# Later batches' mamba with products over 2048 columns, three buffers of decays and two of results

## The reference

```python
x = x + tanh(g_xattn[0]) * mamba(ctx, z=layernorm(x), ...)     # layer 0, "mamba"
x = x + tanh(g_ffn[0]) * bit_linear_ffn(layernorm(x), ...)     # hidden 2048, quantised
x = x + tanh(g_xattn[1]) * attention(layernorm(x), ctx, ...)   # 16 heads of 128 a batch
x = x + tanh(g_ffn[1]) * experts(layernorm(x), ...)            # 4 experts
```

```python
delta = softplus(dt_proj_w @ dt_lo + dt_proj_b); A = -exp(A_log)
# per step t, channel e, state n
dA = exp(delta[e, t] * A[e, n])
state[e, n] = state[e, n] * dA + delta[e, t] * u[e, t] * B[n, t]
y[e, t] += state[e, n] * C[n, t]
y = (y + D * u) * silu(z)
```

## Time and profile before

| | us |
|---|---|
| median of three runs | 1851.22 |
| the profiled execution | 1852.26 |
| its span, first to last instruction | 1850.5 |
| TensorE busy | 1763.2 |
| VectorE busy | 1300.1 |
| ScalarE busy | 963.8 |
| GpSimd busy | 666.5 |

### The profile page before, as it was taken

How to read it: one execution, slowest core, us unless ns; L and a number is a source line. 1 busy time by engine, 2 the same in 40 slices (tenths; PEclk the granted TensorE clock), 3 DMA queues, 4 the chain that set the end, 5 groups by cost and what they waited for, 6 DMA issues and landing times.

```text
span 1850.5 us, 19507 instructions
## 1 busy us (share of the span) xinstructions
PE 1763.2 (95%) x6114; PEld 809.9 (44%) x6114; DVE 1300.1 (70%) x1899; ACT 963.8 (52%) x1920; POOL 666.5 (36%) x696
## 2 busy tenths in 40 slices
PE   8999899879999999999999999999999899999999
PEld 4333344334444444444444444444444344445543
DVE  4989686989998689899787998987652444422221
ACT  7988786446545546566455566555435334320100
POOL 2434322337463324557222564562223333310000
PEclk9999899979999999999999999999999999999999
DMA  7999833767851146897212589732112799837110
GB/s 262 242 289 286 244 109 116 203 164 187 199 142 57 51 100 162 208 240 200 66 30 74 156 188 251 199 95 69 35 57 91 218 282 293 236 119 273 40 51 28
DMA packets 159045, 292.11 MB, mean 158 GB/s; under 512 B 18424, under 2 KB 51704, under 8 KB 156000
## 3 DMA queue, kind: packets, MB, share of 16 engines
q1 hardware_dynamic: 141664, 227.95, 39.0%
q0 software_dynamic: 17280, 62.92, 17.5%
HBM read 169.51 MB, written 58.26 MB: 123 GB/s over the span
## 4 chain that ended last, share of the span: by engine, by line
PE 72%; DVE 13%; ACT 6%; issue 4%; DMA 3%; POOL 1%; SPq 1%; DVEq 0%; ACTq 0%; POOLq 0%
PE p L846 11%; PE p L806 10%; PE p L823 9%; PE p L857 8%; PE p L893 6%; PE p L697 5%; DVE s_M L1025 5%; PE p L780 4%; PE p L829 4%; PE p L908 3%; PE p L746 3%; PE p L785 3%; DVE s_M L1020 2%; DVE s_M L1032 1%; DVE s_U L1178 1%
## 5 line engine op out<-in xcount | busy, mean ns | idle before, releaser
L1025 DVE TENSOR_TENSOR_SCAN s_M<-s_M 128x1024 f32<-128x1024 f32 x128 | 296.4, 2315 | 9.9 <-ACT s_M L1290 7.6
L1178 DVE CUSTOM_DVE_ANT_0 s_U<-p,s_U 128x512 f32<-128x512 f32 x256 | 188.2, 745 | 161.0 <-PE p L823 159.7
L823 PE MATMUL p<-s_U 128*128 128x512 f32 x512 | 268.2, 612 | 4.6 <-DVE s_U L1178 3.0
L806 PE MATMUL p<-s_U 128*128 128x512 f32 x512 | 256.7, 610 | 3.4 <-ACT s_U L1418 2.7
L1534 POOL DMA_DIRECT2D s_u<-s_M x120 | 111.7, 931 | 383.7 <-DVE s_M L1032 355.6
L1579 POOL TENSOR_SCALAR s_U<-s_U 128x512 f32<-128x512 f32 x256 | 231.9, 926 | 6.3
L857 PE MATMUL p<-s_U 128*128 128x512 f32 x512 | 223.7, 593 | 0.0
L846 PE MATMUL p<-s_U 128*128 128x512 f32 x472 | 216.0, 599 | 2.5 <-ACT s_U L1431 2.4
L1431 ACT COPY s_U<-p 128x512 f32<-128x512 f32 x196 | 105.5, 594 | 176.3 <-PE p L829 175.0
L1290 ACT ACTIVATE s_M<-s_dl,s_small 128x511 f32<-128x511 f32 x256 | 170.3, 717 | 35.5 <-DVE s_M L1025 35.3
L1426 ACT ACTIVATE s_U<-s_U 128x512 f32<-128x512 f32 x256 | 181.6, 710 | 5.3
(11 more groups left out here) (194 smaller groups left out, 2458.3 us busy)
## 6 DMA issues: line engine op xcount, KB each, us to landing
s_u<-s_M POOLq DMA_DIRECT2D x120, 512.0 KB, 7.6
s_bc<-bc_scratch SPq DMA_DIRECT2D x96, 256.0 KB, 4.5
k_scratch<-s_U SPq DMA_DIRECT2D x16, 1024.0 KB, 7.9
v_scratch<-s_U SPq DMA_DIRECT2D x16, 1024.0 KB, 5.4
s_U<-in_Wq SPq DMA_DIRECT2D x64, 256.0 KB, 6.6
s_U<-k_scratch SPq DMA_DIRECT2D x64, 256.0 KB, 5.4
s_U<-rk_scratch SPq DMA_DIRECT2D x64, 256.0 KB, 5.8
s_U<-in_Wo SPq DMA_DIRECT2D x64, 256.0 KB, 4.5
```

Source lines behind the costliest of these rows:

```text
L806: ins = e.matmul(banks[bk][:], wqq[j % 2][:, k, :], axT[b % 2][:, k, :], start=(k == 0), stop=(k == 3))
L823: e.matmul(banks[bk][:], qT[j % 3][:, k * 128:(k + 1) * 128], kT[j % 2], start=True, stop=True).then_inc(S["a_s"], 1)
L1025: e.tensor_tensor_scan(w, dA[i % 2], w, 0.0, ALU.mult, ALU.add).then_inc(S["m_s"], 1)
L1178: e.tensor_tensor_reduce(out=Pm[j % 2][:, k, :], in0=banks[ABANK[kind, j, k]][:], in1=rkb[j % 2], scale=rq[:, k:k + 1], scalar=-3.0e38, op ...
```

## The change

For batches 1 to 3 (`wide(b)`): the product with B, that with C and the last addition are one instruction over all four tiles (2048 columns) instead of two over 1024. The scans and decays keep their 1024 columns. There are three decay buffers (`dA3`: the third is what was the third result buffer) and two result buffers of 2048 columns (the second lies where the second `axT` was). A state's two accumulating transfers are issued one behind the other when its whole product with C is done, and both of the state before must have landed. `axT` has one buffer, and batch b's turn waits for the last query of batch b-1. The planner's costs and needs and the semaphore counts follow. Batch 0 keeps its form.

```diff
 def mamba_order(b):
-    ahead = 1 if b else 2
+    ahead = 3 if wide(b) else 2
...
+    if wide(b):
+        for n in range(NS):
+            order += [("mul", n), ("scan", 2 * n)] + ([("decay", 2 * n + 3)] if n < NS - 2 else []) + ([("hn", 0), ("hn", 1)] if n == NS - 1 else [])
+            order += [("scan", 2 * n + 1)] + ([("decay", 2 * n + 4)] if n < NS - 2 else [("decay", last + 1)] if n < NS - 1 else [("hn", 2), ("hn", 3)]) + [("out", n)]
+            order += [("ln", n - NS + 5)] if NS - 6 < n < NS - 1 else []
+        return order + [("add", NS - 1), ("gate", 0), ("gate", 1)] + [("yt", t) for t in range(4)]
...
-            part((kind, i), [("ACT", 1.43)], ("scan", i - (1 if b else 2)) if i >= (1 if b else 2) else ("init", 0))
+            part((kind, i), [("ACT", 1.43)], ("scan", i - (3 if b else 2)) if i >= (3 if b else 2) else ("init", 0))
...
+            if wide(b):
+                part((kind, i), [("DVE", 2.32)], *([("out", i - 2)] if i >= 2 else []))
...
-            part((kind, i), [("DVE", 1.25)] + ([("POOL", 0.8), ("SUM", 5.0)] if i < 2 * NS - 2 else []))
+            part((kind, i), [("DVE", 2.33), ("POOL", 1.8), ("SUM", 6.0)][:3 if i < NS - 1 else 1] if wide(b) else [("DVE", 1.25)] + ([("POOL", 0.8), ("SUM", 5.0)] if i < 2 * NS - 2 else []))
...
-            part(("xxt", t), [("PE", 0.6), ("ACT", 0.7)], ("xhn", t), *([(NB, "q", NH * (b - 1) - 1, 3)] if b > 1 else []), take=[("xt", t)], free=[("xt", t)])
+            part(("xxt", t), [("PE", 0.6), ("ACT", 0.7)], ("xhn", t), *([(NB, "q", NH * b - 1, 3)] if b else []), take=[("xt", t)], free=[("xt", t)])
...
+        wide_y = [M[:, 2048:4096], U[:, 7168:9216]]
+        dA3 = dA + [M[:, 4096:5120]]
...
-        axT = [U[:, o:o + 2048].rearrange("p (k t) -> p k t", k=4) for o in (23552, 7168)]
+        axT = U[:, 23552:25600].rearrange("p (k t) -> p k t", k=4)
...
                     elif kind == "init":
-                        for s in dA:
+                        if wide(b):
+                            e.wait_ge(S["d_bcw"], 16 * b)
+                        for s in dA3 if wide(b) else dA:
...
                     elif kind == "mul":
+                        if wide(b):
+                            e.wait_ge(S[f"d_bc{i % 2}"], 32 * ((NS * (b - 1) + i) // 2 + 1))
+                            if i >= 2:
+                                s, count = term(b, i - 2)
+                                e.wait_ge(S[f"d_w{s}"], count)
+                            if i == 0:
+                                e.wait_ge(S["m_dl"], 2 * b + 2)
+                            e.tensor_tensor(four(wide_y[i % 2]), du[:, :, :], rep(bcs[i % 2][:, 0, :], 4), ALU.mult).then_inc(*v.up())
...
+                    elif kind == "out" and wide(b):
+                        w = four(wide_y[i % 2])
+                        e.wait_ge(S["m_s"], 32 * b + 2 * i + 2)
+                        e.tensor_tensor(w, w, rep(bcs[i % 2][:, 1, :], 4), ALU.mult).then_inc(S["m_c"], 1)
...
-                    if i >= 2:
-                        e.wait_ge(S["m_s"], 32 * b + i - 1)
+                    if i >= (3 if wide(b) else 2):
+                        e.wait_ge(S["m_s"], 32 * b + i - (2 if wide(b) else 1))
...
-                        if t == 0 and b >= 2:
-                            e.wait_ge(S["a_q"], NH * (b - 1))
+                        if t == 0 and b:
+                            e.wait_ge(S["a_q"], NH * b)
...
+                    elif kind == "out" and wide(b):
+                        if i < NS - 1:
+                            if i == 0:
+                                e.wait_ge(S["m_dv"], 4 * b + 4)
+                            e.wait_ge(S["m_c"], states(b, i) + 1)
+                            if i:
+                                last, count = term(b, i - 1)
+                                e.wait_ge(S[f"d_w{last}"], count)
+                            for g in range(2):
+                                e.dma_start(u[:, 2 * g:2 * g + 2, :], four(wide_y[i % 2])[:, 2 * g:2 * g + 2, :], accum_op=ALU.add).then_inc(S[f"d_w{i % 2}"], 16)
...
-                    elif kind == "mul" and b and i % 2 == 0 and i < 2 * NS - 2:
-                        spread(i // 2 + 1)
+                    elif kind == "mul" and b and i < NS - 1:
+                        spread(i + 1)
```

More of the change, by code:

```diff
@@ L67, with wide, states @@
         QUANT += [("bias", 0, k) for k in range(3)]
+def wide(b):
+    return b > 0
+def states(b, i):
+    return 32 * min(b, 1) + NS * max(b - 1, 0) + i
 def mamba_order(b):
-    ahead = 1 if b else 2
+    ahead = 3 if wide(b) else 2
     order = [(k, t) for t in range(4) for k in ("in", "conv")]
@@ L255, in mamba @@
         elif kind == "decay":
-            part((kind, i), [("ACT", 1.43)], ("scan", i - (1 if b else 2)) if i >= (1 if b else 2) else ("init", 0))
+            part((kind, i), [("ACT", 1.43)], ("scan", i - (3 if b else 2)) if i >= (3 if b else 2) else ("init", 0))
         elif kind == "mul":
-            part((kind, i), [("DVE", 1.23)], *([("out", i - NW)] if i >= NW else []), *([("bc", i // 2)] if b == 0 else []))
+            if wide(b):
+                part((kind, i), [("DVE", 2.32)], *([("out", i - 2)] if i >= 2 else []))
+            else:
+                part((kind, i), [("DVE", 1.23)], *([("out", i - NW)] if i >= NW else []), ("bc", i // 2))
         elif kind == "scan":
@@ L261, in mamba @@
         elif kind == "out":
-            part((kind, i), [("DVE", 1.25)] + ([("POOL", 0.8), ("SUM", 5.0)] if i < 2 * NS - 2 else []))
+            part((kind, i), [("DVE", 2.33), ("POOL", 1.8), ("SUM", 6.0)][:3 if i < NS - 1 else 1] if wide(b) else [("DVE", 1.25)] + ([("POOL", 0.8), ("SUM", 5.0)] if i < 2 * NS - 2 else []))
         elif kind == "add":
-            part((kind, i), [("DVE", 1.25)], ("out", i), ("out", i - 2))
+            part((kind, i), [("DVE", 2.33 if wide(b) else 1.25)], ("out", i), ("out", i - 1 if wide(b) else i - 2))
         elif kind == "ln":
@@ L269, in mamba @@
         elif kind == "gate":
-            part((kind, i), [("DVE", 1.3)], ("hn", 2 * i + 1), ("add", 2 * NS - 2 + i))
+            part((kind, i), [("DVE", 1.3)], ("hn", 2 * i + 1), ("add", NS - 1 if wide(b) else 2 * NS - 2 + i))
         elif kind == "yt":
@@ L805, in pe_attn @@
                             e.wait_ge(S[f"d_wq{j % 2}"], 16 * (j // 2 + 1))
-                        ins = e.matmul(banks[bk][:], wqq[j % 2][:, k, :], axT[b % 2][:, k, :], start=(k == 0), stop=(k == 3))
+                        ins = e.matmul(banks[bk][:], wqq[j % 2][:, k, :], axT[:, k, :], start=(k == 0), stop=(k == 3))
                         freed[bk] = (S["a_qs"], j + 1)
@@ L1028, in dve_mamba @@
                         w = two(wy[term(b, i)[0]])
-                        e.wait_ge(S["m_s"], 32 * b + i + 1)
-                        if b == 0 and g == 0:
+                        e.wait_ge(S["m_s"], i + 1)
+                        if g == 0:
                             e.wait_ge(S["m_bc"], 2 * n + 2)
-                        e.tensor_tensor(w, w, rep(bcs[n % 2][:, 1, :] if b else banks[CBANK[n % 2]][:], 2), ALU.mult).then_inc(S["m_c"], 1)
+                        e.tensor_tensor(w, w, rep(banks[CBANK[n % 2]][:], 2), ALU.mult).then_inc(S["m_c"], 1)
+                    elif kind == "add" and wide(b):
+                        s, count = term(b, i - 1)
+                        e.wait_ge(S[f"d_w{s}"], count)
+                        e.wait_ge(S["m_c"], states(b, i) + 1)
+                        e.tensor_tensor(u[:, :, :], u[:, :, :], four(wide_y[i % 2]), ALU.add).then_inc(*v.up())
                     elif kind == "add":
@@ L1285, in decay @@
                     n, g = divmod(i, 2)
-                    av = two(dA[i % 2])
-                    if i >= 2:
-                        e.wait_ge(S["m_s"], 32 * b + i - 1)
+                    av = two(dA3[i % 3] if wide(b) else dA[i % 2])
+                    if i >= (3 if wide(b) else 2):
+                        e.wait_ge(S["m_s"], 32 * b + i - (2 if wide(b) else 1))
                     for t in range(2):
@@ L1528, in pool_mamba @@
                         if i < 2:
-                            e.wait_ge(S["m_dv"], 4 * b + 2 * i + 2)
-                        e.wait_ge(S["m_c"], 32 * b + i + 1)
+                            e.wait_ge(S["m_dv"], 2 * i + 2)
+                        e.wait_ge(S["m_c"], i + 1)
                         if i >= 2:
@@ L1672, in spread @@
                 def spread(n):
-                    kk = NS * b + n
-                    if n >= 2 or b >= 2:
-                        e.wait_ge(S["m_c"], 2 * kk - 2)
+                    if n >= 2:
+                        e.wait_ge(S["m_c"], states(b, n - 1))
+                    elif b >= 2:
+                        e.wait_ge(S["m_c"], states(b - 1, NS - 1 + n))
                     if n == 0 and b:
@@ L1690, in sp_mamba @@
                         spread(0)
-                    elif kind == "mul" and b and i % 2 == 0 and i < 2 * NS - 2:
-                        spread(i // 2 + 1)
```

(6 more changed lines are left out.)

23 lines of the change are left out of this document (14 added, 9 removed).

## The result

The changed kernel takes 1898.03 us (median of four runs, 1893.97 to 1901.51) against 1850.37 (1843.35 to 1852.04) for the kernel before: ratio 1.0264 [1.0226, 1.0303], slower by 48 us. The forecast was 1848, with 1864 as the upper end of its range. The profiled execution has a span of 1899.7 us against 1850.5.

A forecast was written before the change was run, and what follows sets the result against it. TensorE was taken to set the pace, VectorE only from 310 to 382 us; 1 + 1.5 + 1.5 - 0.5 = 3.5 us, rounded to 4, off 1852.26 gave 1848 us, range 1833 to 1864.

The forecast's parts named there:

- Three buffers of decays: Third decay buffer removes most of ScalarE's 35.3 us wait for scans, freeing attention copies behind it; gain 1.5 us (0 to 9.9).
- the long pieces: VectorE's 2048-column products may delay score tiles; the rewritten order may add or remove stalls; 0, ends -5.2 to +16 us.
- The 13.0 us of the earlier trace: One attention head inside mamba takes 13.0 us, set by TensorE, so a faster VectorE (12.5 us of work) can't help.
- Products: VectorE's 2048-column products at 2.29 us save 14.6 us over three batches, of which 1 + 1.5 us reach the path.
- The gain of 1 us from 310 to 382 us: Where VectorE sets the pace beside feed-forward, ten half states save 1.5 us, of which 1 was counted.
- Hardly any ScalarE wait for scans: Sign that the forecast is right: in later batches ScalarE's decays hardly wait for scans any more.
- Sums: Paired accumulating transfers with two result buffers: 9 us of VectorE or GpSimd waits (0 to 40), 0.5 us on the path.
- D: Rival: paired sums landing at 14.3 us slow mamba by 62 us, about 8 showing: 1856; sign GpSimd waits; chance 0.05.
- Turned rows: Single buffer: batch 2's turn moves some 15 us, behind the previous batch's last query, ending 11 us before use; cost 0.
- A: Rival: the VectorE time saved in mamba stretches is on the path after all, 14.6 us less: 1836; chance 0.25.
- B: Rival: 2.29 us products before score tiles make TensorE run out of banks, three to four 5.2 us stalls: 1864; chance 0.15.
- C: Rival: GpSimd's scalings wait behind whole VectorE products, 1.5 us and more each; 10 us: 1858; chance 0.05.

The follow-up runs named there:

- the line put back: Changed kernel, all buffers and run-time waits kept, only the planner again told that a decay needs the scan just before it: 1850.06 us, ratio 1.0005.
- The three pairs: Kernels differing only in the planner's decay need, loosened against tight: 1898.03 and 1850.06 (changed), 1885.3 and the kernel before, 1881.76 and 1847.04 us (1024 columns, three decay buffers).
- 14 us a sum: Changed kernel with the planner told that a state's two sums take 14 us instead of 6: 1879.9 us, ratio 1.0159.
- the later `ln`: Changed kernel with the planner placing the statistics of x's rows two attention heads later in batches 2 and 3: 1883.18 us, ratio 1.0181.
- narrow ones: Kernel before with one turned-rows buffer, three decay buffers, 1024-column products: 1847.04 us with the planner's decay need tight, 1881.76 with it loosened.
- the kernel with a narrow batch 1: Changed kernel with the planner's tight decay need and batch 1 in its old form (1024 columns, two decay, three result buffers): 1845.62 us, ratio 0.9962.
- the kernel before with the loosened need: Kernel before, only decay order changed: two decays ahead in batches 1 to 3, planner told a decay needs the scan before last: 1885.3 us, ratio 1.019.
- the short sums: Changed kernel, same order, each accumulating transfer moving only 16 of 512 columns of each tile: 1896.94 us, ratio 1.0249.
- two short products: Changed kernel with each 2048-column product written as two 1024-column instructions back to back in the same place: 1901.68 us, ratio 1.0279.
- short scalings: GpSimd scales only 128 of 512 columns of each probability tile: 1877.29 us in the changed kernel, 1838.85 with the planner's decay need tight again.

## Why the prediction was wrong

**The step that failed** is "Three buffers of decays ... From 0 to 9.9 us; I take 1.5", with its companion on the long pieces, "the order of everything is written anew by the planner ... 0 in the middle, -5.2 to +16 at the ends". I priced the buffer as a run-time resource and the new order as noise of at most three or four stalls. Yet the diff shows the planner's need going from scan i-1 to scan i-3. The old need was tighter than the two buffers at run time (scan i-2). In the plan it made each half state wait for a decay of 1.43 us after the scan before, and so left gaps in VectorE's order for attention's pieces. The 13.0 us of the earlier trace rows are TensorE's, as I wrote, but only in an order with such gaps: with the line put back most heads beside mamba take 12.9 to 13.6 us, in the changed kernel 15.5 to 18.0 at the place shown. Without it mamba runs ahead in places (10.1 to 10.9 us a state, 14.0 on average over batch 2 for 15.2), heads take up to 18 us, and mamba reaches its `ln` before the rows of x. The three pairs show 48, 36 and 35 us for the order, against my 1.5 us gain. As a run-time resource I had the buffer about right: 0 to 4 us measured.

That the order is the cause is shown. That it costs by mamba running ahead is read from the traces and borne out by the runs with 14 us a sum and with the later `ln`, which each give back only 15 to 18 us.

**Products.** I put 2048 columns at 2.29 us. Measured in the changed kernel, first the products with B, then with C (ns least/median/most):

```profile
L1046 DVE TENSOR_TENSOR s_M<-s_du,s_bc x24: 2271/2284/2592, 314.7 to 1206.2; 128x2048 f32<-128x2048 f32 x24
...
L1066 DVE TENSOR_TENSOR s_M<-s_M,s_bc x24: 2274/2290/2731, 324.6 to 1219.2; 128x2048 f32<-128x2048 f32 x24
```

Right, and so was the saving: added up one by one, products and last additions take 14.8 us less than before, for 14.6 forecast. Yet VectorE's busy time fell by 1.3 us and not by 12 to 16. The scans took 2346 ns in 80 cases and 2383 in 48 for 2315, 5.7 us in all, and VectorE's other instructions 4.1 us more. The last 3.7 us are overlap: in the timeline above a product lasts from 809.24 to 811.51 us and the next instruction begins at 811.43, and with 96 instructions fewer there is less of this. With the line put back the busy time is 1293.4, 6.7 lower. None of it reached TensorE: in the good order long products with two result buffers are some 3 us slower than narrow ones (1850.06 against 1847.04, at the edge of noise), and in the dense one 16 (1898.03 against 1881.76). The gain of 1 us from 310 to 382 us was a loss. TensorE stood 11.0 and 5.5 us for two feed-forward lines there (L763, and L785 from 380 us on), where the same two waits were 5.6 and 5.5 before; with the line put back they are 11.0 and 4.7, and TensorE is busy 55.39 of the 72 us. The kernel with a narrow batch 1 has 59.34, and is 4 us faster than that.

**Decays at run time.** "Hardly any ScalarE wait for scans" came true only with the line put back. The decay's group in that kernel, and then in the kernel before with the loosened need:

```profile
L1336 ACT ACTIVATE s_M<-s_dl,s_small 128x511 f32<-128x511 f32 x256 | 169.8, 719 | 6.0 <-DVE s_M L1062 4.7 <-DVE s_U L1062 1.0
```

```profile
L1290 ACT ACTIVATE s_M<-s_dl,s_small 128x511 f32<-128x511 f32 x256 | 170.2, 715 | 125.5 <-DVE s_M L1025 125.0
```

The four kernels have 6.0 us (need put back), 35.5 (before), 98.6 (changed) and 125.5 (before, loosened). My reading: where plan and run time have the same need, a decay stands in ScalarE's order just when its buffer should come free, and any slip of the scans is waited out there. TensorE's direct waits for ScalarE moved little by it (31.4, 37.9, 40.1 and 40.5 us). From the kernel with the line put back to the changed one TensorE's waits rose by 23.3 us for VectorE, 8.7 for ScalarE and 6.6 for GpSimd, and fell by 2.0 for transfers. What a late ScalarE did to the others is inside these numbers and not separated.

**Sums.** GpSimd stood 42.2 us for sums to land, batch 0's 13.3 among them, against 25.1 before; 17 more, short of the 25 I had named for D. They land in 8.1 us in the median in batches 1 to 3, 8.4 over all 120 (7.6). VectorE stood 8.0 us for them (1.8 before). I had taken 9 us for both engines together, and it is 17.1 + 6.2 = 23.3 more; my lower end for the second of a pair was wrong too (4.5 + 2.7 is 7.2, not 8.5). Rival D is refuted by the short sums.

**Turned rows.** Batch 2's turn stood right behind the last query of the batch before, as forecast: 1088.24 behind 1084.28 us. It cost nothing.

**Rivals.** A (1836) is out: the lowest medians of kernels with all the work done are 1845.6. B had the side right and the mechanism half: more waits for VectorE with a lower clock behind them, but by the place of the pieces, since two short products cost the same; and they fall on the turned probabilities (15.7 us) more than on the score tiles (7.4). C's size, 10 us, came near the 8 to 10 that the dense order adds by the scalings, but by luck: C put it down to whole long products, and the kernel with products of 1024 columns and the loosened need has as much of it. Its sign, scalings of 1.5 us and more, didn't come either (1.016 us on average, 0.926 before).

**What stays open**: how the 38 us that remain with short scalings divide. The later `ln` is worth 15 us alone, but 5 on top of short scalings. Waits taken from one engine came back in part on another. Why sums at 14 us restored batch 1's heads and not batch 2's wasn't settled, nor how much of the difference between two plans is an accident of the planner's choices.

## What to carry to other kernels

Where an order is planned at build time, a dependency in the plan is also a pace: before loosening one because a buffer has come free, ask what it held back, and who filled the gaps. Loosen run time and plan in separate runs; here the resource was worth 0 to 4 us and the line in the plan 35 to 48. A side stream that is needed late may do better at the pace of its host (one state a head) than as fast as its engine allows; of the ways to set that pace tried here, only the tight need gave all of it back.

## What the runs showed of the hardware

GpSimd beside long products on VectorE, in the changed kernel (the products are VectorE's, from 809.24 and 837.13 us):

```profile
809.42 2.14 POOL L1556 TENSOR_SCALAR s_st<-s_st 128x1 f32<-128x1 f32 x1 [4.75 <-DVE s_st L953]
...
824.55 2.34 POOL L1556 TENSOR_SCALAR s_st<-s_st 128x1 f32<-128x1 f32 x1
...
839.14 0.32 POOL L1556 TENSOR_SCALAR s_st<-s_st 128x1 f32<-128x1 f32 x1
```

The two inputs of these products both lie in SBUF. An instruction of one column took 2.14 us beside the product that ran from 809.24 to 811.51, and 2.34 beside the one from 824.55 (2.29 us), but 0.32 us where it began as the third product (837.13, 2.27 us) ended; the median of all 32 is 0.192 us. GpSimd was held until the product was done. The Trainium skill (SBUF — State Buffer, "SBUF: two separate sides") says that of a VectorE instruction with two SBUF inputs and a GpSimd one that reads SBUF, the one that starts first blocks the other for its whole instruction; the trace agrees. What it didn't do here is decide the time: the split products, half as long, cost the same.
